# A fused attention and mixture-of-experts kernel: four chunks of pairs in place of five, and two expert blocks a slot behind the attention

## The chip, the cores and the metric

The kernel runs on one core of one Trainium2 chip. The metric is the device time of one execution in microseconds (us); lower is better. All data is float32. Each product is taken as three matmuls, of a high and a low part of either operand ("hi" and "lo"), so that every operand of TensorE is split first: ScalarE copies the hi part out of PSUM, VectorE subtracts it for the lo part.

## The reference, cut to what matters

Cross-attention over 64 sequences of 128 tokens and then a mixture of experts (two of eight for each token), both with a residual. Cut to the arithmetic:

```python
# attention: 64 sequences, 128 tokens, C = 256, 16 heads of 64
q = layernorm(x) @ Wq;  k, v = split(y @ Wkv)
x = x + softmax(q k^T * 64 ** -0.5) v @ Wproj + bproj
# experts: t = layernorm(x)
probs = softmax(t @ gate_w.T);  top2_w, top2_idx = top_k(probs, 2)
mixed = sum over the two chosen e of top2_w * silu(t @ expert_w[e].T + expert_b[e])
x = x + mixed @ combine_w.T
```

## The kernel before, in words

**Pairs and slots.** The 64 sequences are worked in 32 pairs (256 tokens each). The attention of a pair takes 8 slots, one for each pair of heads; slot s belongs to pair s // 8 and has u = s % 8. All engines walk the same list of slots in program order, each issuing its own part, and meet at semaphores. The attention fills slots 0 to 255; what comes from slot 256 on is called the tail here.

**Two ways through the experts.** The last four pairs (28 to 31) are "dense": all eight experts are computed for all their tokens, in 32 dense jobs (`plan.dense`, 8 a pair, up to 3 a slot, from slot 256 on). A dense job is 6 matmuls of 512 columns into one of four banks (`dense_ps`); ScalarE takes tanh and scales, VectorE multiplies (`dense_out`) and adds (`dense_add`), GpSimd adds (`add_odd`).

The first 28 pairs (`SPARSE`) are "sparse", in chunks of `CHUNKS` = 8, 8, 6, 4, 2 pairs. After the last pair of a chunk its rows lie sorted by expert in `sorted_x` (scattered by GpSimd), and a chunk of n pairs is worked in 4n + 7 blocks of 128 rows (`Plan.blocks`), the 7 being room for the padding of eight experts: 39, 39, 31, 23 and 15, together 147. `Plan.turn` gives each block a slot, one block a slot.

**A block turned in slot s:** SyncE loads its rows in slot s-2 (`load_rows`, 128 KB) and its expert's weights in s-1 (`load_expert`, 512 KB); TensorE turns the rows in slot s (`turn_block`, L714, 2 matmuls, "early" in the slot), the two splits go to `xbT`; in s+1 TensorE does 6 matmuls (`expert`, "late"); in s+2 ScalarE does tanh and VectorE `expert_out` (L1089) into `y_block`; in s+3 SyncE stores the block to `sorted_y` (`store_block`, L503). The rings of `x_block`, `w_block` and `y_block` have three places (`RING`), `xbT` has two. The waits of the rings: `load_rows(n)` on `turn_block` n-3, `load_expert(n)` on `expert` n-3, `expert_out(n)` on the landed store of block n-3.

**Mixing a sparse pair m:** when all blocks of its chunk are stored, GpSimd gathers four times (`gather`, indirect DMAs; two buffers, so that the first gather of pair m waits for `turn_mixed` of pair m-2), ScalarE weighs (`weigh`, L938), TensorE sums and turns (`turn_mixed`, L681, 8 matmuls) and one slot later multiplies (`combine`, 12 matmuls), VectorE adds the residual (`combined`, L1095) that SyncE has loaded back (`x1_back`), SyncE stores. `Plan.mix` gives the slot: mixes at s, `turn_mixed` in s+1, `combine` in s+2, `combined` in s+3.

**Banks.** All jobs beside the attention's own (`value`, `turn_x`, `turn_x1`, `gate`, `rank`, `turn_block`, `expert`, `turn_mixed`, `combine`) take three PSUM banks `gen_ps` in turn, in the order of `Plan.order`: a job waits until the job three before it is drained (`before_in_bank`).

**Order inside a slot of the tail.** TensorE: `turn_block`, then `turn_x1`/`gate`/`turn_mixed` ("mid"), then `expert`, `combine` ("late"), then the dense jobs. VectorE: `expert_out`, `combined`, then `dense_out` and `dense_add` of the dense jobs of slot s-1, then the lo splits of `turn_block` and of `turn_mixed`. GpSimd: `add_odd` of slot s-1's dense jobs and the gathers, alternately. SyncE: `load_rows`, `load_expert`, `store_block`, (the expert table for the dense jobs, 4 x 512 KB each, in slots 253 and 256: `load_experts`), the store of the output, the load of `x1_back`.

**The plan before, by slots:** blocks turned in 78 to 116, 142 to 180, 190 to 220, 222 to 244 and 245 to 259 (143 of them below slot 256, 4 in the tail; the chunks end with pairs 8, 16, 22, 26, 28, and behind each end VectorE computes the block list in the pair after the next). `turn_mixed` of pairs 0 to 21 lies below slot 256, of 22 to 27 in the tail, the last two (26, 27) mixed at slots 266 and 268. The last dense job stands in slot 267.

## Time and profile before

| | |
|---|---|
| median of the runs | 1540.31 us (1539.81 to 1540.96, 3 runs) |
| the profiled execution | 1538.33 us |
| its span, first to last instruction | 1536.6 us |
| PE (TensorE) busy | 1489.9 us, 97% |
| DVE (VectorE) busy | 1291.6 us, 84% |
| ACT (ScalarE) busy | 1061.8 us, 69% |
| POOL (GpSimd) busy | 939.1 us, 61% |
| granted TensorE clock | 0.996 of full speed |

The profile names instructions by line of the kernel, engine, and the tiles written and read. SP is SyncE. The tail is read from the order of time of each engine; for the attention, stretches of one pair each are read, each cut at the first of the four transposes of the probabilities (L636) that open a slot on TensorE. The names in the trace are those of the memory: `xT` and `v_s` can be the turned rows of a dense pair, `wq_s`, `wkv_s` the dense expert weights, and `x_kept` the kept residual.

### The profile page before, as it was taken

To read this page: it belongs to the slowest core of one execution; us is meant where nothing else is said; L and a number is where in the kernel's file an instruction comes from. 1 tells how busy PE (TensorE), PEld (TensorE's weight loads), DVE (VectorE), ACT (ScalarE), POOL (GpSimd) and SP (SyncE) were. 2 spreads that over 40 slices of the span, in tenths; PEclk is the share of its full clock that TensorE was granted. 3 is DMA by queue.
4 is the path that set the end of the run, shared out by engine and by line. 5 is a ranking of instruction groups with operands and counts; after the bars stand their busy time and mean duration, and the time that the engine had idled before them with its cause. 6 is when DMAs were issued, how large, how long until landed. Compare 5 with 4: busy or idle time off the path is not lost.

```text
span 1536.6 us, 38493 instructions
## 1 busy us (share of the span) xinstructions
PE 1489.9 (97%) x11680; PEld 1433.8 (93%) x11680; DVE 1291.6 (84%) x3129; ACT 1061.8 (69%) x2929; POOL 939.1 (61%) x1237
## 2 busy tenths in 40 slices
PE   6989999999999999999999999999999999999898
PEld 6989999999899999999999999989999999999887
DVE  7888888888988888888988888888888888987677
ACT  5766776766677667676677667766767667677665
POOL 4666666666655555587766455657666656655644
PEclk8999999999999999999999999999999999999999
DMA  6643443333577777544578777647887778887853
GB/s 183 201 152 94 108 110 97 94 94 97 162 226 209 220 217 223 159 114 140 172 230 244 217 231 232 203 117 220 243 250 237 230 228 248 251 243 216 285 183 110
DMA packets 181596, 287.78 MB, mean 187 GB/s; under 512 B 23697, under 2 KB 116881, under 8 KB 181137
## 3 DMA queue, kind: packets, MB, share of 16 engines
q1 hardware_dynamic: 170640, 255.94, 57.0%
q0 software_dynamic: 10752, 29.37, 6.1%
q8 instruction: 97, 1.59, 0.5%
q14 instruction: 107, 0.87, 0.2%
HBM read 156.51 MB, written 61.60 MB: 142 GB/s over the span
## 4 chain that ended last, share of the span: by engine, by line
PE 77%; DVE 14%; issue 3%; ACT 2%; SPq 2%; DMA 1%; POOL 0%; DVEq 0%; ACTq 0%; POOLq 0%
PE gen_ps L595 20%; PE qk_ps L595 17%; PE o_ps L595 10%; PE s_ps L595 10%; PE proj_ps L595 9%; PE pT_ps L636 6%; DVE sums L1073 2%; PE gen_ps L714 2%; PE gen_ps L681 2%; DVE neg_max L1066 2%; DVE pT_s_lo L1008 1%; DVE qk_s L1008 1%; PE gen_ps L689 1%; DMA k_s<-qk_s 1%; DVE xn L1053 1%
## 5 line engine op out<-in xcount | busy, mean ns | idle before, releaser
L851 ACT ACTIVATE stage<-s_ps,neg_max 128x128 f32<-128x128 f32 x1024 | 293.7, 376 | 32.1 <-DVE neg_max L1066 31.1
L1405 POOL CAST o_s_hi<-stage 128x256 fp32r<-128x256 f32 x256 | 102.5, 400 | 342.8 <-ACT stage L825 340.9
L1396 POOL TENSOR_TENSOR stage<-stage,inv_sums 128x512 f32<-128x512 f32 x256 | 266.1, 1039 | 36.8 <-DVE inv_sums L1075 36.4
L825 ACT CAST qk_s<-qk_ps 128x512 fp32r<-128x512 f32 x256 | 150.8, 589 | 134.3 <-PE qk_ps L595 132.7
L1066 DVE TENSOR_REDUCE neg_max<-s_ps 128x4 f32<-128x512 f32 x256 | 176.4, 689 | 66.6 <-PE s_ps L595 62.4
L595 PE MATMUL s_ps<-k_s,qk_s 128*128 128x256 f32 x1536 | 226.7, 284 | 2.8 <-DMA k_s<-qk_s 2.2
L1008 DVE TENSOR_TENSOR pT_s_lo<-pT_ps,pT_s_hi 128x512 fp32r<-128x512 f32 x256 | 173.7, 678 | 45.7 <-ACT pT_s_hi L825 41.4
L595 PEld LDWEIGHTS s_ps<-k_s,qk_s 128*128 128x128 f32 x1536 | 201.8, 189 | 3.5 <-DMA k_s<-qk_s 2.8
L1407 POOL TENSOR_TENSOR o_s_lo<-stage,o_s_hi 128x256 fp32r<-128x256 f32 x256 | 189.4, 740 | 20.8
L825 ACT CAST v_s_hi<-gen_ps 128x512 fp32r<-128x512 f32 x129 | 75.8, 588 | 179.4 <-PE gen_ps L595 179.4
L825 ACT CAST pT_s_hi<-pT_ps 128x512 fp32r<-128x512 f32 x256 | 150.4, 588 | 64.4 <-PE pT_ps L636 60.3
L1073 DVE TENSOR_REDUCE sums<-stage 128x4 f32<-128x512 f32 x256 | 172.6, 674 | 24.6 <-ACT stage L851 23.6
L825 ACT COPY stage<-o_ps 64x256 f32<-64x256 f32 x512 | 187.9, 367 | 3.1
L1008 DVE TENSOR_TENSOR qk_s<-qk_ps,qk_s 128x512 fp32r<-128x512 f32 x256 | 174.5, 681 | 0.5 <-ACT qk_s L825 0.4
L595 PE MATMUL o_ps<-pT_s_hi,v_s_hi 128*128 128x256 f32 x512 | 155.9, 304 | 18.7 <-DVE pT_s_lo L1008 18.4
L595 PE MATMUL qk_ps<-xT_hi,wq_s_hi 128*128 128x256 f32 x512 | 165.2, 323 | 7.9 <-DVE cT_hi L1060 4.0
L636 PE MATMUL pT_ps<-ident,stage 128*128 128x128 f32 x1024 | 154.5, 273 | 1.2 <-POOL stage L1396 1.1
L595 PE MATMUL proj_ps<-wproj_s_hi,o_s_hi 128*128 128x256 f32 x512 | 144.9, 283 | 2.0 <-POOL o_s_lo L1407 2.0
L595 PE MATMUL o_ps<-pT_s_hi,v_s_lo 128*128 128x256 f32 x512 | 145.2, 284 | 0.0
L595 PE MATMUL o_ps<-pT_s_lo,v_s_hi 128*128 128x256 f32 x512 | 144.7, 283 | 0.0
L595 PE MATMUL qk_ps<-xT_hi,wq_s_lo 128*128 128x256 f32 x512 | 144.7, 283 | 0.0
L595 PE MATMUL proj_ps<-wproj_s_hi,o_s_lo 128*128 128x256 f32 x512 | 144.3, 282 | 0.0
(385 smaller groups left out, 4695.2 us busy)
## 6 DMA issues: line engine op xcount, KB each, us to landing
w_block<-expert_table SPq DMA_DIRECT2D x147, 512.0 KB
k_s<-qk_s SPq DMA_DIRECT2D x512, 128.0 KB
stage<-sorted_x SPq DMA_DIRECT2D x147, 128.0 KB
sorted_y<-stage SPq DMA_DIRECT2D x147, 128.0 KB, 4.0
x_raw<-in_x SPq DMA_DIRECT2D x32, 256.0 KB
c_raw<-in_ctxT SPq DMA_DIRECT2D x32, 256.0 KB, 3.9
stage<-in_x SPq DMA_DIRECT2D x32, 256.0 KB, 3.7
x_kept<-x SPq DMA_DIRECT2D x32, 256.0 KB
```

The source lines that it names most:

```text
L595: mm = pe.matmul(out_ap, l, r, start=start and n == 0, stop=stop and n == len(terms) - 1, skip_group_check=skip)
L636: mm = pe.transpose(pT_ps[:, k * P:(k + 1) * P], probs[p % 2][:, k, :], ident[:, :])
L681: mm = pe.matmul(bank[:, a * N2 + t * P:a * N2 + (t + 1) * P], rows(t, k)[:, a * P:(a + 1) * P], ident[:, :], is_transpose=True, start=k = ...
L714: mm = pe.transpose(bank[:, a * P:(a + 1) * P], x_block[n % RING][:, a * P:(a + 1) * P], ident[:, :])
L825: last = act.copy(to, of)
L851: last = act.activation(probs[p % 2][:, k, :], s_ps[:, k * P:(k + 1) * P], ACT.Exp, bias=neg_max[p % 2][:, k:k + 1])
L1008: last = dve.tensor_tensor(lo, of, hi.bitcast(F32), ALU.subtract)
L1066: dve.tensor_reduce(neg_max[p % 2][:, :], s_ps[:, :].rearrange("p (k n) -> p k n", k=4), AX_X, ALU.max, negate=True).then_inc(max_done, 1)
L1073: dve.tensor_reduce(sums[p % 2][:, :], probs[p % 2][:, :, :], AX_X, ALU.add).then_inc(sums_done, 1)
L1396: pool.tensor_tensor(probs[b][:, :, :], probs[b][:, :, :], inv_sums[b][:, :].unsqueeze(2).broadcast_to([P, 4, P]), ALU.mult).then_inc(prob ...
L1405: pool.tensor_copy(hi[:, :, :], o_full).then_inc(o_hi, 1)
L1407: pool.tensor_tensor(lo[:, :, :], o_full, hi[:, :, :].bitcast(F32), ALU.subtract).then_inc(o_lo, 1)
```

## The change

The chunks are 9, 9, 7 and 3 pairs, so the blocks are 43, 43, 35 and 19, together 140. From slot 256 on the plan takes two blocks a slot. Blocks turned in slot 256 or later ("late") put their hi and lo parts in four places in `qk_s`, which the attention no longer uses, and not in the two of `xbT`. SyncE loads rows of late blocks one slot ahead and their weights in their own slot (before: two slots and one slot ahead), and in the tail stores the blocks of slot s-3 ahead of the loads rather than behind them. Everything else follows from `Plan`.

The new plan by slots: blocks turned in 86 to 128, 158 to 200, 214 to 248 and 249 to 261 (128 below slot 256; 12 in slots 256 to 261, two a slot). `turn_mixed` of pairs 0 to 17 below slot 256; pairs 18 to 27 in the tail, with mixes of 24, 31, 25, 26, 27 at slots 267, 268, 269, 271, 273. The last dense job stays in slot 267. The gathers of pairs 25, 26 and 27 stand in slots 266, 268 and 270.

The jobs on the three banks in the first slots of the tail, in order (before: `turn_block`, `turn_mixed` and `expert` of one block each in slot 256, for example):

```
256: turn_block 128, turn_block 129, turn_mixed, expert 127
257: turn_block 130, turn_block 131, expert 128, expert 129, combine
258: turn_block 132, turn_block 133, turn_mixed, expert 130, expert 131
259: turn_block 134, turn_block 135, expert 132, expert 133, combine
260: turn_block 136, turn_block 137, turn_x1, turn_mixed, expert 134, expert 135
261: turn_block 138, turn_block 139, gate, turn_mixed, expert 136, expert 137, combine
262: turn_mixed, expert 138, expert 139, combine
```

```diff
-CHUNKS = (8, 8, 6, 4, 2)
+CHUNKS = (9, 9, 7, 3)
...
             for b in range(self.blocks[c]):
-                self.turn[at] = (c, b, self.first[c] + b)
-                at += 1
+                while len(self.turn.get(at, [])) >= (1 if at < SLOTS * pairs else 2):
+                    at += 1
+                self.turn.setdefault(at, []).append((c, b, self.first[c] + b))
...
+        self.late_blocks = [n for at, jobs in self.turn.items() if at >= SLOTS * pairs for _, _, n in jobs]
...
+        late_xbT = [[qk_s[b // 2][:, b % 2, part, :].rearrange("p (a n) -> p a n", a=2) for part in range(2)] for b in range(4)]
+        turned = lambda n: late_xbT[n % 4] if n in plan.late_blocks else whole(xbT[n % 2])
...
-                if s + 2 in plan.turn:
-                    load_rows(*plan.turn[s + 2])
-                if s + 1 in plan.turn:
-                    load_expert(*plan.turn[s + 1])
-                if s - 3 in plan.turn:
-                    store_block(*plan.turn[s - 3])
+                if s - 3 >= SLOTS * pairs:
+                    for job in plan.turn.get(s - 3, []):
+                        store_block(*job)
+                for at, load, late in ((s + 2, load_rows, False), (s + 1, load_rows, True),
+                                       (s + 1, load_expert, False), (s, load_expert, True)):
+                    if (at >= SLOTS * pairs) == late:
+                        for job in plan.turn.get(at, []):
+                            load(*job)
+                if s - 3 < SLOTS * pairs:
+                    for job in plan.turn.get(s - 3, []):
+                        store_block(*job)
...
                     elif kind == "turn_block":
-                        wait(act, made["expert"], n - 1)
...
+                        if n not in plan.late_blocks:
+                            wait(act, made["expert"], n - 1)
+                        elif n - 4 in plan.late_blocks:
+                            act.wait_ge(made["expert"], n - 3)
+                        else:
+                            act.wait_ge(s_made, pairs * HEAD_PAIRS)
```

## Rows read from the trace of the kernel before

**Rows 1.** The page: span, and busy time of the engines.

```profile
span 1536.6 us, 38493 instructions
PE 1489.9 (97%) x11680; PEld 1433.8 (93%) x11680; DVE 1291.6 (84%) x3129; ACT 1061.8 (69%) x2929; POOL 939.1 (61%) x1237
```

**Rows 2.** Stretches, one pair each: length, PE, PEld, DVE, ACT, POOL busy, clock, DMA share, GB/s.

```profile
344.92:383.92 39.00, 38.22 (x305) 36.96 (x304) 33.84 (x80) 27.38 (x76) 24.98 (x34) 1.00 0.37 96
383.92:426.53 42.61, 40.21 (x314) 37.99 (x313) 38.81 (x104) 28.89 (x80) 25.23 (x34) 1.00 0.56 162
471.75:516.96 45.21, 45.21 (x368) 44.30 (x367) 38.72 (x97) 31.68 (x92) 25.16 (x34) 1.00 0.75 222
690.35:733.84 43.49, 42.70 (x345) 41.47 (x344) 35.82 (x85) 31.43 (x87) 32.99 (x43) 1.00 0.48 134
830.53:880.73 50.20, 50.05 (x408) 48.88 (x407) 41.64 (x101) 35.75 (x104) 25.45 (x35) 1.00 0.76 226
1304.65:1356.06 51.41, 50.25 (x406) 48.65 (x405) 44.96 (x114) 35.56 (x102) 33.24 (x43) 1.00 0.83 255
1406.23:1451.03 44.80, 42.87 (x354) 41.73 (x352) 33.00 (x81) 32.95 (x98) 26.32 (x35) 1.00 0.81 248
```

**Rows 3.** PE in order of time, tail: start, length, instruction, idle before it and releaser.

```profile
1453.57 0.41 PE L714 MATMUL gen_ps<-ident,stage 128*128 128x128 f32 x2 [1.94 <-DMA stage<-sorted_x]
...
1462.22 0.40 PE L595 MATMUL gen_ps<-w_block,xbT_hi 128*128 128x256 f32 x2
...
1462.94 0.28 PE L595 MATMUL gen_ps<-wcomb_s_hi,mT_s_hi 128*128 128x256 f32 x1
...
1464.36 0.39 PE L595 MATMUL pT_ps<-wq_s_hi,x1T_hi 128*128 128x512 f32 x1
...
1467.15 0.38 PE L714 MATMUL gen_ps<-ident,stage 128*128 128x128 f32 x2
...
1473.44 0.38 PE L714 MATMUL gen_ps<-ident,stage 128*128 128x128 f32 x2
1473.58 0.48 PE L595 MATMUL gen_ps<-w_block,xbT_hi 128*128 128x256 f32 x2
```

**Rows 4.** Page, costliest groups: a 128x512 copy out of PSUM on ScalarE (mean ns of one).

```profile
L825 ACT CAST pT_s_hi<-pT_ps 128x512 fp32r<-128x512 f32 x256 | 150.4, 588 | 64.4 <-PE pT_ps L636 60.3
```

**Rows 5.** VectorE in order of time, tail (columns as in Rows 3).

```profile
1455.15 0.42 DVE L1089 SCALAR_TENSOR_TENSOR stage<-stage,gen_ps 128x256 f32<-128x256 f32 x1 [2.12 <-DMA sorted_y<-stage]
...
1467.68 0.69 DVE L1095 TENSOR_TENSOR stage<-gen_ps,stage 128x512 f32<-128x512 f32 x1 [3.70 <-DMA stage<-x_kept]
...
1470.27 0.42 DVE L1008 TENSOR_TENSOR xbT_lo<-gen_ps,xbT_hi 128x256 fp32r<-128x256 f32 x1
```

**Rows 6.** SyncE in order of time, tail: loads of weights, of rows, stores.

```profile
1450.12 0.34 SPq L498 DMA_DIRECT2D w_block<-expert_table  x1
1450.50 0.46 SPq L503 DMA_DIRECT2D sorted_y<-stage  x1
1451.95 0.34 SPq L486 DMA_DIRECT2D stage<-sorted_x  x1
```

**Rows 7.** The stores of blocks (L503) from 1440 us on: issue to landing.

```profile
DMA to landing us min/median/max: 3.2/4.6/6.3
```

**Rows 8.** Stretches of one slot of the tail, columns as in Rows 2.

```profile
1451.03:1459.64 8.61, 6.67 (x47) 5.86 (x46) 3.64 (x10) 3.87 (x9) 4.81 (x7) 1.00 1.06 389
1473.44:1479.98 6.54, 6.54 (x40) 5.66 (x39) 4.80 (x10) 4.93 (x12) 5.55 (x7) 1.00 0.26 81
```

**Rows 9.** The end, by engine in order of time: last dense matmul, gathers, weighing, last addition.

```profile
1524.83 0.40 PE L595 MATMUL o_ps<-wkv_s_hi,v_s_lo 128*128 128x512 f32 x1
...
1518.80 0.95 POOL L1441 DMA_INDIRECT stage<-sorted_y,y_row_of  x1 [0.30 <-issue]
...
1525.76 1.69 ACT L938 ACTIVATE stage<-stage,top_w 128x256 f32<-128x256 f32 x4
...
1533.28 0.69 DVE L1095 TENSOR_TENSOR stage<-gen_ps,stage 128x512 f32<-128x512 f32 x1 [0.70 <-PE gen_ps L595]
```

More of the change, by code:

```diff
@@ L115, in __init__ @@
                     mid.append((kind, (i + off) * per(kind) + k))
-            if s in self.turn:
-                early.append(("turn_block", self.turn[s][2]))
+            for _, _, n in self.turn.get(s, []):
+                early.append(("turn_block", n))
             if s - 1 in self.mix:
                 mid.append(("turn_mixed", self.mix[s - 1]))
-            if s - 1 in self.turn:
-                late.append(("expert", self.turn[s - 1][2]))
+            for _, _, n in self.turn.get(s - 1, []):
+                late.append(("expert", n))
             if s - 2 in self.mix:
@@ L719, in expert @@
                 pe.wait_ge(w_block_in[n % RING], 16 * (n // RING + 1))
-                xs, w = xbT[n % 2], w_block[n % RING]
+                xs, w = turned(n), w_block[n % RING]
                 terms = []
@@ L901, in general @@
                     elif kind == "turn_block":
-                        wait(act, made["expert"], n - 1)
-                        to = xbT[n % 2][0][:, :, :].rearrange("p a n -> p (a n)")
-                        split_hi(made[kind], n + 1, [(to, bank[:, 0:N2])], hi_of[kind])
+                        if n not in plan.late_blocks:
[4 more added lines that the diff above has]
+                            act.wait_ge(s_made, pairs * HEAD_PAIRS)
+                        split_hi(made[kind], n + 1, [(turned(n)[0], bank[:, 0:N2].rearrange("p (a n) -> p a n", a=2))],
+                                 hi_of[kind])
                     elif kind == "turn_mixed":
@@ L963, in _ @@
                     pT(i, u - 1)
-                if s - 2 in plan.turn:
-                    tanh(plan.turn[s - 2][2])
+                for _, _, n in plan.turn.get(s - 2, []):
+                    tanh(n)
                 todo = plan.dense.get(s - 1, [])
@@ L1263, in general @@
                     elif kind == "turn_block":
-                        hi, lo = (y[:, :, :].rearrange("p a n -> p (a n)") for y in xbT[n % 2])
-                        split_lo(hi_of[kind], n + 1, [(lo, bank[:, 0:N2], hi)], drained[kind])
+                        hi, lo = turned(n)
+                        split_lo(hi_of[kind], n + 1, [(lo, bank[:, 0:N2].rearrange("p (a n) -> p a n", a=2), hi)], drained[kind])
                     elif kind == "gate":
@@ L1294, in _ @@
                     add_residual(i - 1)
-                if s - 2 in plan.turn:
-                    expert_out(plan.turn[s - 2][2])
+                for _, _, n in plan.turn.get(s - 2, []):
+                    expert_out(n)
                 if s - 3 in plan.mix:
```

## The prediction

> **What bounds the kernel now.** I read the page first, then stretches of one pair each, then each engine in order of time in the tail, and last the end.
>
> TensorE is busy 1489.9 of 1536.6 us [rows 1]. In the attention the stretches show it directly. A pair without blocks takes 39.00 us, one with 8 blocks 45.21 with PE busy for all of it, one with 2 mixes and no block 43.49, one with both 50.20 [rows 2]. So work taken from TensorE there shortens the kernel at its full price. The exceptions are the pairs in which VectorE computes a block list: 42.61 with two blocks, where 39.00 plus two blocks would be 40.6 [rows 2]; about 2 us are lost at each chunk end.
>
> The tail runs from 1451.03, the start of slot 256 [rows 8], to 1536.6, so 85.6 us. Its beginning is disturbed by DMA: share 1.06 and PE busy 6.67 of 8.61 us in slot 256, with a wait of 1.94 us for a block's rows; by slot 259 the share is 0.26 and PE is busy throughout [rows 3, 8]. The last dense matmul ends at 1524.83 + 0.40 = 1525.2 and 11.4 us of mixes, addition and output follow [rows 9].
>
> **Term 1, the attention.** The plan's counts with the stretches [rows 2] as prices. One block costs (45.21 - 39.00) / 8 = 0.78 us, two mixes 4.5 to 5.0. Pairs 8 to 31 last 1451.03 - 344.92 = 1106.1 us before. After, they are: two without anything (78.0), a chunk end with 2 blocks (42.6), five with 8 blocks (226.1), one with a single block (39.8), two with mixes only (87.0), a chunk end with 2 blocks and 2 mixes (42.6 + 4.5 = 47.1), one full (50.2), one with 8 blocks and a mix (47.7), three with 8 blocks (135.6), one with a block (39.8), a chunk end as above (47.1), two full (100.4), a chunk end with 8 blocks and 2 mixes (51.4), one with 8 blocks and a mix (47.7), and the last pair, which is 44.80 before and loses both mixes (39.8). Sum 1080.2, so -26. By parts: 15 blocks fewer are -11.6, four mixes -9 to -10, one chunk end -2, which is -23; the rest is from fewer slots in which blocks and mixes meet. I take -26, with -23 and -28 as bounds.
>
> **Term 2, work moved into the tail.** Eight blocks and four mixes more than before (12 blocks turned and 13 `expert` against 4 and 5; 10 sparse mixes against 6). A turn is 0.14 us (1473.44 to 1473.58), an `expert` 0.72 (1462.22 to 1462.94), a `combine` 1.42 (1462.94 to 1464.36), a mix as a whole 2.25 to 2.5 (half of the 4.5 to 5.0 above), which leaves some 0.87 for its `turn_mixed` [rows 2, 3]. Eight blocks are 6.9 us. Ahead of the end of the last dense job only one of the four mixes lies (0.87 + 1.42 = 2.3), the others fall behind it. So +9.2 up to there.
>
> **Term 3, the end.** Before, three `turn_mixed`/`combine` are still open behind the last dense job, and the last gather was issued at 1518.80, long before. After, pairs 24, 31, 25, 26 and 27 are open, and the gather of 26 waits for `turn_mixed` of 24, that of 27 for `turn_mixed` of 25, both behind the last dense job. Counted from its end: the last dense job's tanh (0.6, as the copy of the same shape [rows 4]), `dense_out` (0.7), scaling and `add_odd` stand ahead of the gather on GpSimd, 2.9 with a split between them; four gathers of 0.95 + 0.30 [rows 9] are 5.0, twice, so the last begins at 12; landing 3.5 (estimate from the stores' 3.2 to 4.6 [rows 7]); weighing 1.7; `turn_mixed` 1.1, the two splits 1.3 (0.59 and 0.69 [rows 4, 9]), `combine` 1.6; addition and output from 1533.28 to 1536.6, 3.3 [rows 9]. That is 24.7 against 11.4: +13.3. If the gathers were hidden only PE's work would count: 5 x 0.87 + 6 x 1.42 + 3.3 = 16.2, so +4.8. I take +13.3, because the waits are in the code and nothing is left that could cover them.
>
> Without new stalls the sum is -26 + 9.2 + 13.3 = -3.5.
>
> **Term 4, new waits of two blocks a slot.** Three banks and a job that waits for the third before it: with one block a slot `expert` waits for jobs of the slot before. With two, in slot 259, `expert` 133 waits until `turn_block` 134 of its own slot is drained; `turn_mixed` waits in the same way in 260 and 261, `combine` for `turn_mixed` in 262. The lo split that drains it stands on VectorE behind the dense jobs of the slot before. Rows: in slot 258, start 1467.15, it begins at 1470.27, 3.1 us in [rows 3, 5]; PE would need the bank after 1.0 us (two turns and one `expert`). Queued behind the waiting matmul are the dense jobs, so the stall is not hidden.
>
> How late is it? From `combined` at 1467.68 to that split are 2.6 us with two dense jobs, so 1.0 us a dense job [rows 5]. Lower bound: VectorE keeps up and only the last dense job is left at the slot's start (tanh 0.6, then 1.0, the addition of the job before it 0.4, the split 0.42): drained at 2.4, a stall of 1.4, four times, 5.5 us. Upper bound: VectorE is held by the ring of `y_block`. `expert_out` of a slot's second block needs the store that SyncE issues at the head of the same slot, and SyncE gets there only after the weights' load that waits for the first `expert` of the slot before. That load, a store and its next issues take 0.4 to 1.45 us each [rows 6], together about 2.5, and the store lands in 4.6 [rows 7]: 7.1 after that `expert`, where TensorE needs 0.7 + 4.2 (+1.4) = 4.9 to 6.3 to the next slot (the 4.2 are three dense jobs, two of them lasting from 1464.36 to 1467.15 [rows 3]). So `expert_out` is held 0.8 to 2.2 us into the slot and three dense jobs (3.0), the addition and the split follow: drained at 4.5 to 6, stalls of about 3.5, four times 14 us. The same kind of wait exists in slot 256 before, 2.12 us for `sorted_y` [rows 5].
>
> The first slots add to it. In 256 `turn_mixed` now waits for the bank that this `expert_out` (1455.15) drains, and the rows of the second block are asked for only one slot ahead in a full DMA: +2.5. In 258 `turn_mixed` waits for `combined`, which waited for `x_kept` until 1467.68 [rows 5]: +2.5. The four places for turned rows remove a wait that costs nothing here. Term 4 is then 10 to 19 us; I take 14.
>
> **A rule weighed.** The rows show stores landing in 3.2 to 6.3 us, median 4.6 [rows 7]. The Trainium skill (DMA: Bandwidth & Descriptors, Anatomy of one DMA) puts the fixed cost of a DMA at some 2 us, most of it the write's receipt. By that rule the store would land before it is missed and term 4 would be its lower bound, 10, so 1547; the rows were taken with the DMA engines full, as they will be here, so I go by the rows.
>
> **The sum.** -26 + 9.2 + 13.3 + 14 = +10.5 on the profiled execution's 1538.3 gives 1548.8. The median of the runs lies 2.0 above the profiled one: 1550.8, so 1551.
>
> **Rivals.**
> (B) The banks and the ring are hidden: VectorE and SyncE keep ahead and term 4 is 0 to 3. For it: VectorE has idle time in slot 258 (3.70) [rows 5] and is 84% busy in all [rows 1]. Against it: the order in which the lo split comes last. Time: 1540.3 - 3.5 + 1 = 1538; with term 1 at -28, 1536. This is the side "not slower".
> (C) The end isn't bound by gathers: term 3 is +4.8. Time with term 4: 1542; with a small term 4, 1530. For it: GpSimd is 61% busy [rows 1]. Against: the two waits named.
> (D) DMA binds. Eight blocks more are 8 x 768 KB = 6.3 MB. At slot 256's 389 GB/s with share 1.06 [rows 8] that is 16 us of full engines, against 8 us more of PE work. It decides if the loads of slots 256 to 259 (with the 2 MB of the expert table) aren't through by slot 260; weights then land late, and term 4 grows to about 24: 1561.
> That the change doesn't do what it says isn't a case for itself: the block count falls from 147 to 140 by the plan. If moved work were free in the tail, term 1 alone would stand, 1514; TensorE's full slots there [rows 8] exclude it.
>
> **Chances.** Forecast 0.52, B 0.20, C 0.13, D 0.15. About 0.2% (3.1 us) is what a measurement of this kernel can tell from no change. The forecast is slower but for 0.04; B is faster 0.08, same 0.11, slower 0.01; C 0.04, 0.04, 0.05; D slower. Together faster 0.12, same 0.19, slower 0.69. The range, 1537 to 1562, leaves out the low ends of B and C and the worst of D.
>
> **What would show it.** Term 1: slot 256 starts near 1425. Term 2: five slots from 256 with two `turn_block` each. Term 3: from the last dense matmul to the end some 25 us, with eight gathers in it one after the other. Term 4: in slots 259 to 262 idle time ahead of `gen_ps` matmuls, released by VectorE's `xbT` lo or by `expert_out`, and VectorE waiting for `sorted_y`. I am wrong if PE is as busy there as in slot 259 before, or if the end is as short as 16 us.

## The result, and the profile after

The changed kernel takes 1578.45 us (median of 4 runs, 1573.81 to 1582.06) against 1540.63 for the kernel before in the same session, a ratio of 1.0244 [1.0222, 1.0266]. So it is slower, as forecast, but by 38 us where 10.5 were forecast, and outside the range. The profiled execution took 1577.42 us, its span 1575.7. The rows of its page that answer to [rows 1]:

```profile
span 1575.7 us, 38156 instructions
PE 1500.7 (95%) x11624; PEld 1441.6 (91%) x11624; DVE 1282.6 (81%) x3096; ACT 1057.4 (67%) x2915; POOL 938.2 (60%) x1237
```

PE has 56 matmuls fewer and is busy 10.8 us longer. Something makes matmuls longer, which no step of the prediction provided for.

The span is cut here at three points: the first transposes of the probabilities in slot 24 (the start-up is over by then), those of slot 256, and the end of the last dense matmul. All values are us from the profiled executions. "Last gather" is the start of the last indirect DMA against the last dense matmul.

| kernel | slot 24 at | 24 to 256 | 256 to last dense | from there to the end | last gather | median | ratio to before |
|---|---|---|---|---|---|---|---|
| before | 149.9 | 1301.2 | 74.2 | 11.4 | -6.4 | 1540.6 | 1 |
| after | 156.0 | 1280.8 | 111.5 | 27.5 | +12.4 | 1578.45 | 1.0244 |
| forecast | as before | 1275 | 97.4 | 24.7 | +12 | 1551 | |
| e1 chunks only | 148.9 | 1279.9 | 92.8 | 36.1 | +23.5 | 1559.4 | 1.0129 |
| e5 two a slot only | 148.5 | 1304.8 | 85.3 | 11.7 | -27.1 | 1552.4 | 1.0080 |
| e2 output places | 155.4 | 1283.6 | 96.8 | 29.0 | +12.4 | 1558.4 | 1.0131 |
| e4 own banks | 149.2 | 1280.5 | 104.6 | 29.6 | +12.4 | 1565.6 | 1.0169 |
| e6 both | 152.1 | 1281.3 | 94.0 | 27.9 | +12.4 | 1549.9 | 1.0050 |
| e3 weights a slot later | 148.5 | 1281.7 | 117.6 | 27.2 | +12.4 | 1577.4 | 1.0249 |
| e7 e6, weight places | 149.7 | 1280.0 | 92.8 | 27.6 | +12.4 | 1551.4 | 1.0070 |
| e8 e7, gathers free | 155.4 | 1279.7 | 91.6 | 26.8 | +10.5 | 1555.7 | 1.0114 |
| e9 waits filled | 154.0 | 1280.8 | 117.5 | 27.9 | +12.4 | 1578.2 | 1.0247 |
| e10 9, 9, 6, 4 | 149.8 | 1289.9 | 87.2 | 16.9 | +3.0 | 1544.9 | 1.0023 |
| e11 the same, code before | 151.4 | 1290.5 | 78.3 | 29.9 | +13.5 | 1549.5 | 1.0050 |
| e12 e10, output places | 148.6 | 1288.2 | 85.9 | 16.9 | +3.0 | 1541.3 | 1.0001 |
| e13 e12, rows early, a stall | 150.9 | 1290.6 | 85.2 | 18.1 | +3.0 | 1545.8 | 1.0028 |
| e14 rows early, no stall | 150.1 | 1288.0 | 80.4 | 16.8 | +3.0 | 1539.1 | 0.9992 |

The attention gained 20.4 of the 26 us forecast. The stretch to the last dense matmul lost 37.3 (forecast 23.2), the end 16.1 (forecast 13.3). The start-up took 6.1 us more; that isn't the change (see the last section).

The stretch to the last dense matmul as one line, of before and then of after (length, PE, PEld, DVE, ACT, POOL busy, granted clock, DMA share, GB/s):

```profile
1451.03:1525.22 74.19, 70.83 (x414) 60.58 (x412) 55.83 (x115) 46.94 (x105) 38.54 (x48) 1.00 0.53 176
1436.75:1548.22 111.47, 91.51 (x500) 78.60 (x499) 61.83 (x133) 55.77 (x130) 44.76 (x54) 0.88 0.57 181
```

TensorE is idle there for 20.0 us in place of 3.4, and busy for 20.7 us more. So the 37.3 us are 16.6 of waiting and 20.7 of busy time; the second part is moved work and matmuls at a lower granted clock (below).

**The waits.** VectorE in order of time in the tail of after (start, length, instruction, idle before it and releaser), the lines that answer to the first of [rows 5]:

```profile
1459.38 0.42 DVE L1105 SCALAR_TENSOR_TENSOR stage<-stage,gen_ps 128x256 f32<-128x256 f32 x1 [9.65 <-DMA sorted_y<-stage]
1469.88 0.42 DVE L1105 SCALAR_TENSOR_TENSOR stage<-stage,gen_ps 128x256 f32<-128x256 f32 x1 [5.12 <-DMA sorted_y<-stage]
1480.82 0.42 DVE L1105 SCALAR_TENSOR_TENSOR stage<-stage,gen_ps 128x256 f32<-128x256 f32 x1 [2.53 <-DMA sorted_y<-stage]
1496.81 0.42 DVE L1105 SCALAR_TENSOR_TENSOR stage<-stage,gen_ps 128x256 f32<-128x256 f32 x1 [6.76 <-DMA sorted_y<-stage]
1510.21 0.42 DVE L1105 SCALAR_TENSOR_TENSOR stage<-stage,gen_ps 128x256 f32<-128x256 f32 x1 [3.69 <-DMA sorted_y<-stage]
```

`expert_out` stands and waits for the landed store of the block three before it: 27.8 us in five waits, where before had 2.8 in two. SyncE in order of time shows why the stores are late (answering to [rows 6]):

```profile
1452.59 0.34 SPq L504 DMA_DIRECT2D w_block<-expert_table  x1
1452.97 0.43 SPq L509 DMA_DIRECT2D sorted_y<-stage  x1
1454.17 3.76 SPq L492 DMA_DIRECT2D stage<-sorted_x  x2
1458.72 6.80 SPq L504 DMA_DIRECT2D w_block<-expert_table  x2
1465.56 0.43 SPq L509 DMA_DIRECT2D sorted_y<-stage  x1
```

The two weight loads take from 1458.72 to 1465.52, since the second waits for TensorE's `expert` three blocks back; the store stands behind it in the same queue. The first and longest of the five waits, 9.65 us, isn't of this kind: its store, issued at 1452.97, stood behind loads that waited for no `expert`, and took 6.31 us to land. The `expert` that holds the second weight load is in PE's list (columns as above):

```profile
1456.18 0.66 PE L725 MATMUL gen_ps<-ident,stage 128*128 128x128 f32 x2 [3.10 <-DMA stage<-sorted_x]
1459.85 0.69 PE L725 MATMUL gen_ps<-ident,stage 128*128 128x128 f32 x2 [3.01 <-DVE stage L1105]
...
1462.77 2.93 PE L606 MATMUL gen_ps<-w_block,qk_s 128*128 128x256 f32 x12 [0.35 <-DVE qk_s L1024]
...
1473.07 1.64 PE L606 MATMUL gen_ps<-w_block,qk_s 128*128 128x256 f32 x6 [2.27 <-DVE stage L1105]
1476.95 1.65 PE L606 MATMUL gen_ps<-w_block,qk_s 128*128 128x256 f32 x6 [2.23 <-DVE qk_s L1024]
```

TensorE waits for L1105, which is `expert_out` again. That closes a circle: `expert` frees the weights' place, SyncE issues the load and only then the store, the store lands, `expert_out` runs and drains the bank, the next `turn_block` and `expert` run. The first `expert` of a slot starts at 1462.77, 1473.07, 1487.99, 1502.78 and 1512.68. The four periods between (columns as in the fence of the whole stretch):

```profile
1462.77:1473.07 10.30, 8.03 (x34) 6.69 (x34) 2.77 (x9) 2.70 (x6) 6.26 (x8) 0.83 0.66 215
1473.07:1487.99 14.92, 11.29 (x59) 9.89 (x59) 10.71 (x22) 8.18 (x20) 3.18 (x4) 0.77 0.45 127
1487.99:1502.78 14.79, 9.81 (x54) 8.61 (x52) 5.85 (x14) 4.78 (x11) 5.44 (x6) 0.80 0.60 195
1502.78:1512.68 9.90, 9.90 (x53) 9.04 (x51) 3.58 (x7) 5.13 (x12) 0.96 (x2) 0.77 0.38 124
```

TensorE is idle for 2.3, 3.6, 5.0 and 0.0 us of them, and in each about 2 us of its busy time are there because the clock is low (busy time times what is missing of the clock, an estimate). The remaining 6 to 9 us are work. Only the first and the third period go over the weights and a store. In the second the chain that ended last runs over VectorE instead: the multiplications and additions of the dense jobs stand ahead of the lo split of the turned rows (`qk_s`, L1024) that TensorE waits for, 2.23 and 1.40 us. That is the wait that term 4 described.

**The clock.** Stretches of 10 us of after (length, PE, PEld, DVE, ACT, POOL busy, granted clock, DMA share, GB/s):

```profile
1446.70:1456.70 10.00, 6.70 (x41) 5.41 (x39) 2.45 (x7) 4.04 (x11) 1.36 (x2) 0.97 1.08 362
1456.70:1466.70 10.00, 6.64 (x27) 5.57 (x27) 5.27 (x13) 2.80 (x7) 1.62 (x3) 0.52 0.43 141
1466.70:1476.70 10.00, 5.74 (x26) 4.32 (x24) 4.46 (x9) 4.25 (x11) 6.27 (x7) 0.82 0.96 303
1496.70:1506.70 10.00, 7.42 (x34) 7.33 (x35) 5.84 (x13) 5.04 (x13) 2.37 (x3) 0.52 0.16 54
```

Behind the stretches in which TensorE idles, the granted clock falls to 0.52, close to the lower of the two levels (1.2 of 2.4 GHz), and 27 matmuls keep PE busy for 6.64 us where 41 took 6.70 in the stretch ahead. The twelve matmuls of two `expert` at 1462.77 took 2.93 us; at the full clock two take 0.87 and 0.95. This is the likely source of the 10.8 us more of PE busy time: busy time times what is missing of the clock comes to some 9.6 us up to the last dense matmul and 2.5 behind it, where before has nothing (an estimate). Whether that busy time is also lost time is what e9 asks.

### The profile page after: what moved, and what is told of

The parts are those of the page before. It is cut to its first block, busy times and chain, and to the rows that moved or that the text cites. A ratio compares the mean times of both kernels' runs of the same rounds, so it can differ in the third digit from the quotient of the medians.

```text
span 1575.7 us, 38156 instructions
## 1 busy us (share of the span) xinstructions
PE 1500.7 (95%) x11624; PEld 1441.6 (91%) x11624; DVE 1282.6 (81%) x3096; ACT 1057.4 (67%) x2915; POOL 938.2 (60%) x1237
## 4 chain that ended last, share of the span: by engine, by line
PE 75%; DVE 13%; issue 4%; DMA 3%; ACT 2%; SPq 2%; POOL 1%; DVEq 0%; ACTq 0%; POOLq 0%
PE gen_ps L606 19%; PE qk_ps L606 17%; PE o_ps L606 10%; PE s_ps L606 10%; PE proj_ps L606 9%; PE pT_ps L647 6%; PE gen_ps L725 2%; PE gen_ps L692 2%; DVE sums L1089 2%; DVE neg_max L1082 1%; DVE pT_s_lo L1024 1%; DVE qk_s L1024 1%; DMA k_s<-qk_s 1%; PE gen_ps L700 1%; DVE xn L1069 1%
## 5 line engine op out<-in xcount | busy, mean ns | idle before, releaser
L862 ACT ACTIVATE stage<-s_ps,neg_max 128x128 f32<-128x128 f32 x1024 | 292.9, 375 | 29.6 <-DVE neg_max L1082 28.5
L1024 DVE TENSOR_TENSOR pT_s_lo<-pT_ps,pT_s_hi 128x512 fp32r<-128x512 f32 x256 | 173.5, 678 | 44.0 <-ACT pT_s_hi L836 39.3
L1024 DVE TENSOR_TENSOR qk_s<-qk_ps,qk_s 128x512 fp32r<-128x512 f32 x256 | 174.3, 681 | 0.4 <-ACT qk_s L836 0.4
L606 PE MATMUL qk_ps<-xT_lo,wq_s_hi 128*128 128x256 f32 x512 | 144.4, 282 | 0.0
```

Source lines behind the costliest of these rows:

```text
L606: mm = pe.matmul(out_ap, l, r, start=start and n == 0, stop=stop and n == len(terms) - 1, skip_group_check=skip)
L862: last = act.activation(probs[p % 2][:, k, :], s_ps[:, k * P:(k + 1) * P], ACT.Exp, bias=neg_max[p % 2][:, k:k + 1])
L1024: last = dve.tensor_tensor(lo, of, hi.bitcast(F32), ALU.subtract)
```

## The experiments

**e1 and e5: each half of the change alone.** e1 is the code before with the new chunks, e5 the changed code with the old chunks.

```diff
-CHUNKS = (8, 8, 6, 4, 2)
+CHUNKS = (9, 9, 7, 3)
```

> The kernel before with the chunks 9, 9, 7, 3 and nothing else: one block a slot in the tail too. Theory R (the ring of y_block with two blocks a slot makes the tail slow): VectorE no longer waits for sorted_y by more than some 3 us in all, the tail up to the last dense job is 74 + 9 = 83 us in place of 111.5, the end is longer (the last block is stored in slot 270, then three pairs are gathered): some 30 us. Attention as in the changed kernel. Total 1545 to 1552. Theory P (the chunk plan itself, more mixes and gathers in the tail, makes it slow): 1565 or more.

> The changed kernel with the old chunks 8, 8, 6, 4, 2: two blocks a slot only for the four blocks of slots 256 and 257. Theory R (ring of y_block) and B (banks) both: few slots have two blocks, so 2 to 8 us of new waits; the attention as before (T, the start of slot 256, at 1451 in a run with the short start), the end not longer than 11.4 us because pairs 26 and 27 are mixed earlier. Total 1541 to 1548. If two blocks a slot cost nothing by themselves: 1540 or less.

The chunks alone bring the whole gain in the attention (1279.9) and lose it in the tail: 92.8 and 36.1, since one block a slot ends in slot 267 and the last gather comes 23.5 us behind the last dense matmul. The median, 1559.4, lies between the two theories (1552 at most, 1565 at least): VectorE waits for stores 0.6 us only, as theory R has it, but TensorE waits seven times, 6.8 us in all, for the lo split of the turned rows (`xbT_lo`), which neither theory had. Two blocks a slot alone cost 11.1 us up to the last dense matmul (2 to 8 were expected) though only four blocks are late. VectorE's waits for stores there, in e5:

```profile
DVE stage L1105 <- DMA sorted_y<-stage: 10.8, 3, 9.0
```

(us in total, times, longest). TensorE itself waits twice there, 5.3 us for this `expert_out` and 3.4 for rows. So the ring is the larger part of the price of two a slot, and not all of it; and both halves are slower than before. What the second half buys is the end: 27.5 in place of 36.1.

**e2, e4, e6: the ring and the banks.** e2 gives the outputs of the 12 late blocks places of their own in `k_s`, so that `expert_out` waits for no store. e4 takes the late `turn_block` from slot 258 on out of the three banks, into halves of `proj_ps`. e6 is both.

```diff
+        y_late = [k_s[b][:, h, part, :] for b in range(AHEAD) for h in range(2) for part in range(2)]
...
-                wait(dve, y_stored[n % RING], 16 * (n // RING))
+                if n in plan.late_blocks:
+                    dve.wait_ge(s_made, pairs * HEAD_PAIRS)
+                else:
+                    wait(dve, y_stored[n % RING], 16 * (n // RING))
```
```diff
+            if plan.own_bank((kind, n)):
+                return proj_ps[:, (n % 2) * N2:(n % 2 + 1) * N2]
```

> The changed kernel, but the outputs of the 12 late blocks have a place each in the keys' buffers, so that expert_out waits for no store (these outputs are rounded to the matmul's input format, which changes no work). Theory R: the 28 us that VectorE waits for sorted_y vanish; the tail falls from 139 to 110 to 115 us, total 1550 to 1555. Theory B (the bank coupling of turn_block and expert inside a slot is the cause): 5 us at most are gained, total 1572 or more, with the idle time of TensorE now all released by the lo split.

> The changed kernel, but the turned rows of late blocks from slot 258 on use the two halves of the projection's bank, which is free by then, so that no expert or turn_mixed waits for a turn_block of its own slot. Theory B: 15 us or more gained, total 1563 or less. Theory R: 2 to 6 us gained, total 1572 to 1576, and VectorE's waits for sorted_y stay near 28 us.

> The changed kernel with both of the edits tried one at a time: own places for the outputs of late blocks, and the projection's bank for their turned rows from slot 258 on. If ring and banks are two separate delays: T to the last dense matmul falls from 111.5 to 88 to 92 us (the work alone needs 83), total 1548 to 1552. If one is only behind the other in the same chain: no better than the places alone, 96.8 us and 1556 or more.

Up to the last dense matmul: 111.5, with places 96.8, with banks 104.6, with both 94.0. So the ring is worth 14.7 alone and 10.6 on top of the banks, the banks 6.9 alone and 2.8 on top of the places. Together 17.5 us of the 37.3. With the waits goes the low clock: in e6 TensorE is idle for 10.1 us and busy for 83.9, at a granted clock of 0.98, so that 7.6 of the 17.5 us are busy time. e2 and e6 fell short of what was expected of them (a median of 1558.4 against 1550 to 1555, and 94.0 us against 88 to 92). Each is a link of the circle; taking out either shortens it, the ring much more.

**e3: the order on SyncE.** The second block's weights are loaded a slot later, behind the stores and the rows.

```diff
+                if s - 1 >= SLOTS * pairs:
+                    for job in plan.turn.get(s - 1, [])[1:]:
+                        load_expert(*job)
```

> The changed kernel, but SyncE issues the weights of a slot's second late block one slot later, behind the stores and the loads of rows, so that a store no longer stands behind a load that waits for TensorE's expert. The ring of y_block keeps three places. Theory R in its narrower form (the store waits in SyncE's queue): 12 to 20 us gained, total 1558 to 1566. If the landing of the stores is what counts: under 5 us gained. Theory B: nothing.

TensorE's waits in its tail:

```profile
PE gen_ps L612 <- DMA w_block<-expert_table: 15.9, 4, 7.3
```

The store no longer stands behind the weights, but now the weights come late: 117.6, and none of the 12 to 20 us expected is gained. The order alone moves the wait and doesn't take it away. I put that down to the rings, with three places where two blocks a slot want more under way; no run shows it by itself.

**e7 and e8: the weights' ring and the gathers.** e7 adds eight places for late weights to e6. e8 adds to that a place of its own for pair 26's gathered rows, so that the gathers of 26 wait for no `turn_mixed`, and issues those of 26 one slot and of 27 two slots earlier.

```diff
-                    if m >= 2:
-                        pool.wait_ge(made["turn_mixed"], plan.turn_of[m - 2] + 1)
+                    if m >= 2 and m != SPARSE - 2:
+                        pool.wait_ge(made["turn_mixed"], plan.turn_of[m - (3 if m == SPARSE - 1 else 2)] + 1)
```

> As e6, and the weights of the late blocks in eight places (three of w_block, the third part of qk_s, four in the projection's weights) in place of three, so that SyncE's loads wait for no expert of the slot before. If the order of SyncE still holds the tail: 3 to 6 us less than e6, T to the last dense matmul at 84 to 86. If DMA bandwidth holds the first slots: no change against e6.

> As e7, and pair 26 is gathered into the place of x_block (free by then) one slot earlier, pair 27 two slots earlier into pair 26's place, so that neither waits for a turn_mixed behind the last dense job. If the end is bound by gathers one after the other: from the last dense matmul to the end 29 falls to 20 to 23 us, total 6 to 8 us below e7. If TensorE or the splits bind the end: 2 us or less.

e7 moves the stretch by 1.2 us (3 to 6 were expected) and the median not at all: with the outputs free, the weights were hardly late. e8, expected at 20 to 23 us for the end and measured at 26.8, is the miss that tells most about it. Its last dense matmul ends at 1526.70, and GpSimd in order of time is

```profile
1519.60 0.97 POOL L1509 DMA_INDIRECT stage<-sorted_y,y_row_of  x1 [4.37 <-PE gen_ps L732]
1520.59 0.75 POOL L1519 TENSOR_TENSOR last_row<-last_row,stage 128x256 f32<-128x256 f32 x1
...
1532.58 0.73 POOL L1519 TENSOR_TENSOR zero_rows<-zero_rows,c_raw 128x256 f32<-128x256 f32 x1
...
1537.25 0.94 POOL L1509 DMA_INDIRECT stage<-sorted_y,y_row_of  x1 [0.30 <-issue]
```

From 1519.60 on GpSimd has no pause: 12 gathers and six additions stand in one line, and the last gather still starts 10.5 us behind the last dense matmul. The earlier gathers now stand ahead of the additions that the last dense pair needs, and PE waits for the one at 1532.58. So at the end it is GpSimd's queue that binds, not the wait that was removed.

**e9: is the low clock a cause?** 90 matmuls whose results nobody reads are put into TensorE's waits of the tail.

```diff
+                for _ in range(count):
+                    pe.matmul(to[:, 0:2 * C], wcomb_s[0][:, 0, 0:P],
+                              wcomb_s[0][:, :, :].rearrange("p a n -> p (a n)"), start=True, stop=True)
```

> The changed kernel with matmuls that compute nothing used put into TensorE's waits of the tail: 11 ahead of turn_block 132 and of turn_block 133 (slot 258), 8 ahead of expert 132 and of expert 133 (slot 259), 5 ahead of turn_mixed in slot 260, 11 ahead of the gate and 7 ahead of turn_mixed in slot 261, and behind the dense jobs 3, 10 and 10 ahead of the last three turn_mixed and 6 and 6 ahead of the last two combines; 90 matmuls of 512 columns, some 0.235 us each at the full clock (dense jobs of the trace: six from 1546.65 to 1548.06), 21 us in all, each lot a little shorter than the wait in which it lies. Theory 'the low clock is part of the circle': in the changed kernel TensorE's granted clock falls to 0.52 in 1456.7 to 1466.7 and in 1496.7 to 1506.7, 0.82 and 0.84 between; its busy time times what is missing from 1 gives 3.2 + 1.0 + 1.4 + 3.6 = 9 us of real work lengthened. With the waits filled the clock stays near 1 and slot 256 to the last dense matmul goes from 111.5 to about 102, and the end (clock 0.76 and 0.84) from 27.5 to about 25.5: median 1567. Rival 'the clock is only a trace of the waits': the work in the clock's low stretches is hidden behind the waits for stores and banks, and the fillers at best cost nothing: 111 to 116 us and 27 to 29, median 1578 to 1584.

Stretches of e9, the first two for those of after at 0.52 and 0.82:

```profile
1454.80:1464.80 10.00, 7.77 (x38) 5.63 (x36) 3.19 (x7) 2.20 (x7) 0.00 (x0) 1.00 0.83 290
1464.80:1474.80 10.00, 8.12 (x42) 6.60 (x42) 2.62 (x9) 2.36 (x5) 6.25 (x8) 1.00 0.68 223
1494.80:1504.80 10.00, 7.62 (x37) 5.88 (x36) 4.74 (x11) 1.93 (x5) 1.66 (x2) 0.83 0.42 154
```

The clock stays at the full level in the first two periods and falls again later (0.90 and 0.81 in the third and fourth). In sum nothing is gained: 117.5 us, of which 3.2 are a longer wait for rows in slot 256, where nothing was filled (4.78 against 1.59). The four periods are 10.1, 13.6, 15.9 and 9.5 us against 10.3, 14.9, 14.8 and 9.9 in after.

- The first shows that the low clock isn't what made it long: at the full clock it is as long as before, since VectorE waits for a store until 1474.59, and the `expert` that needs the bank starts at 1475.07.
- The second is 1.3 us shorter, the third 1.1 longer; there VectorE waited 7.91 us for a store, where it waited 6.76 in after.
- In the fourth TensorE waits for nothing in either run, and the clock is low in both (0.81 and 0.77). What a full clock would give there, e9 doesn't show.
- Behind the last dense matmul e9 is no test. Ten fillers stand ahead of the last `turn_mixed`, where after has no wait, and two lots of fillers, 2.28 and 2.31 us, lie on the chain that ended last. That the end is as long as in after (27.9 against 27.5) can be a shorter end with fillers in it.

So the low clock isn't the main cause of the waits. What it costs by itself stays open: it isn't shown to be free.

**e10, e11, e12: the third chunk one pair shorter.** Chunks of 9, 9, 6 and 4 have the same 140 blocks, but the third chunk's 31 blocks start in slot 206, not 35 in slot 214, so only 5 blocks are late and not 12. e10 is the changed code, e11 the code before, e12 is e10 with the output places of e2.

```diff
-CHUNKS = (9, 9, 7, 3)
+CHUNKS = (9, 9, 6, 4)
```

> The changed code with chunks of 9, 9, 6 and 4 pairs in place of 9, 9, 7 and 3. The same 140 blocks, but the third chunk ends a pair earlier, so only 5 blocks are left for the tail (slots 256 to 258, of which 256 and 257 take two) instead of 12, and 20 pairs are mixed below slot 256 instead of 18; the gathers of pair 27 stand in slot 267, its mix in 270 (before: 268). Theory 'what costs is how much is late and how late': attention -13 by the prices of the stretches (8 blocks fewer 6.2, two mixes 4.7, a chunk end 2), of which experience with 9, 9, 7, 3 leaves about -10; to the last dense matmul +3 of work (one block 0.9, about one mix 2.3) and +4 of waits in the two double slots; the end +3 to +6 for mixes that stand two slots later. Sum 0 to +3: 1540 to 1543. Rival 'the fourth chunk and the code behind it cost by themselves' (two blocks a slot at the full price of the run with two a slot alone, +12 to the last dense matmul, and an end of 25 us or more): 1555 or more.

> The code before (one block a slot) with chunks of 9, 9, 6 and 4: 140 blocks, 5 in the tail, one a slot in 256 to 260. The mix of pair 27 stands in slot 273, five slots later than before, and the gathers of 25, 26 and 27 in 266, 268 and 270. Attention -10 as in the run above. To the last dense matmul +3 of work and no ring or bank waits. Theory 'the end is bound by when the last gathers come': last gather about 12 us behind the last dense matmul and an end near 27 as in the changed kernel, +16; sum +9: 1549. Rival 'the end only follows from its work' (two mixes more behind the dense jobs, some 5 us): 1539.

> As the changed code with chunks 9, 9, 6, 4, and with places of their own for the outputs of the five late blocks (rounded to the type of those places), so that VectorE's expert_out waits for no store in the tail. With 9, 9, 7, 3 these places were worth 14.7 us to the last dense matmul, for 12 late blocks and five waits. Here only the waits at the first double slots are left to remove: the theory of the ring gives -2 to -5 against the run without them. If the ring matters only where doubles follow each other for six slots: no difference, within 1 us.

e10 came near what the first theory said (1540 to 1543): 1544.9, within 5 us of the kernel before and 34 us below the changed kernel. e11 shows what two blocks a slot are good for: it wins 8.9 us up to the last dense matmul against e10 and loses 13 at the end, with the last gather at +13.5 in place of +3.0. e12 takes 1.3 us off that stretch and 3.6 off the median; the first is less than I expected (2 to 5), since TensorE's waits for rows grew from 4.6 us in e10 to 8.0 as those for `expert_out` went.

**e13 and e14: what the rows wait for.** In e12 TensorE (first fence) waits twice for rows, and SyncE (second fence) had issued the rows of the first wait behind the table of the dense experts:

```profile
1442.09 1.09 PE L728 MATMUL gen_ps<-ident,stage 128*128 128x128 f32 x4 [4.72 <-DMA stage<-sorted_x]
...
1460.84 0.41 PE L728 MATMUL gen_ps<-ident,stage 128*128 128x128 f32 x2 [3.30 <-DMA stage<-sorted_x]
```
```profile
1426.34 0.39 SPq L524 DMA_DIRECT2D wq_s_hi<-expert_table  x1
...
1434.25 1.47 SPq L494 DMA_DIRECT2D stage<-sorted_x  x2
```

Both runs load the late rows earlier, in free places. The lines are those of e14; e13 asked for four of the rows in slot 253 and for the fifth in slot 254.

```diff
+                if s == SLOTS * pairs - 3:
+                    for job in plan.turn[SLOTS * pairs]:
+                        load_rows(*job)
+                if s == SLOTS * pairs - 1:
+                    for job in plan.turn[SLOTS * pairs + 1] + plan.turn[SLOTS * pairs + 2]:
+                        load_rows(*job)
```

> As the run with chunks 9, 9, 6, 4 and places for the outputs, and with the rows of the late blocks loaded before the 2 MB of the dense experts' table and not behind it: blocks 135 to 138 in slot 253, 139 in slot 254, in places of x_block whose blocks are turned by then and in the place of the chosen experts' masks, which is free after the last block list. Theory 'the rows queue behind the table': in the run without it the rows of 135 and 136 were issued at 1434.25, behind the four loads of the table from 1426.34 on, and TensorE waited 4.72 us for them at 1442.09; those of 139 were issued behind the second half of the table and TensorE waited 3.30 us at 1460.84. Both waits go; the weights that follow in the same full queues may give 1 to 3 of the 8 us back. Slot 256 to the last dense matmul from 85.9 to 79 to 81 us; median 1534.5 to 1537, which is faster than the kernel before. Rival 'the engines of DMA are the bound in slots 253 to 258, whatever the order': the weights come as much later as the rows come earlier, 84 to 87 us and 1540 to 1542.

> The run with the rows early again, without the wait that spoilt it. There SyncE asked in slot 253 for a place of x_block whose block is only turned in slot 254; it stood in the rows' load from 1426.85 to 1435.63 and issued the table at 1437.33 instead of 1426.34, and TensorE then waited 8.20 us for the first late block's weights' work. Now the rows of 135 and 136 go in slot 253, ahead of the table, to the place of the chosen experts' masks, with no wait, and those of 137, 138 and 139 in slot 255, where block 134 has been turned by the time SyncE comes there (1432.59 against 1434.25). Theory 'the rows queue behind the table': the waits of 4.72 and 3.30 us go, some 1 to 3 come back as waits for weights; slot 256 to the last dense matmul 79 to 82 us against 85.9, median 1535 to 1538, ratio about 0.997. Rival 'DMA is the bound in slots 253 to 258': 84 to 87 us, 1540 to 1542, ratio 1.000.

e13 fell into the trap that it was to study. SyncE of e13, then of e14:

```profile
1426.85 8.78 SPq L501 DMA_DIRECT2D stage<-sorted_x  x5
...
1437.33 0.39 SPq L532 DMA_DIRECT2D wq_s_hi<-expert_table  x1
```
```profile
1425.05 2.59 SPq L501 DMA_DIRECT2D stage<-sorted_x  x3
...
1429.35 0.39 SPq L532 DMA_DIRECT2D wq_s_hi<-expert_table  x1
```

One of the five loads of e13 asked for a place whose block was turned a slot later, and the table moved back by 11 us behind it. Without that stall, e14 goes from slot 256 to the last dense matmul in 80.4 us (expected 79 to 82; e12 85.9), and no wait of TensorE for rows is left there (one of 3.62 us for `expert_out` in slot 256 is). The bytes to be moved are the same in both runs, so what the rows of e12 waited for was their place in the order, not the bandwidth. The median, 1539.14, ratio 0.9992 [0.9977, 1.0006], is 1 us above what was expected and can't be told from the kernel before: long chunks can be had at no loss, but I found no version that is faster.

## Why the prediction was wrong, point by point

**Term 1, attention: right in kind, 5.6 us too high.** 20.4 of 26. Slot 256 came at 1436.7, or 1430.6 counted without the late start-up, against 1425 forecast. Two stretches of after for [rows 2], columns as there (the pair for which 45.21 was used, and one with everything):

```profile
1063.00:1108.16 45.16, 45.16 (x369) 44.26 (x367) 38.73 (x97) 31.65 (x92) 25.16 (x34) 1.00 0.77 221
1195.78:1246.01 50.23, 50.08 (x408) 48.86 (x407) 41.53 (x100) 35.19 (x100) 33.38 (x43) 1.00 0.79 239
```

The prices held. The excess lies in pairs to which I gave the price of an undisturbed one: 40.9, 40.7 and 40.9 where a single block was put at 39.8, and 48.4 and 52.0 at chunk ends put at 47.1 and 51.4; together 4.9.

**Term 2, moved work: some 2 us too low.** TensorE's busy time in the stretch, at the full clock, is 70.8 us before and about 82 after (91.5 less the 9.6 above; e7, with a clock of 0.98, is at 83.4). That is 11 us of work against 9.2, by an estimate.

**Term 4, the waits: this is the step that failed.** 37.3 - 9.2 leaves 28 where term 4 had 14. What the runs show in its place has two parts.

The idle time itself came near: 16.6 us more than before, against 14. It isn't spread as forecast. "Stalls of about 3.5, four times" are idle times of 2.3, 3.6, 5.0 and 0.0 us, and from slot 256 up to the first of them TensorE was idle for 8.4 us, where the 3.4 of before and the 5 forecast for the first slots make the same. The mechanism was named rightly: `expert_out` held by the landed store, which SyncE issues behind the load that waits for `expert`, and the lo split behind the dense jobs. That the sum nearly fits is in part luck: the fourth stall didn't come, the third was longer, and VectorE's longest wait, 9.65 us, was for a store that took 6.31 us to land and had no `expert` in its way. A part of the two in the middle isn't explained by a run: in both, a job of pair 31 (`turn_x1`, `gate`) and a `turn_mixed` stand in the order of the banks too.

The larger part of what is missing is a term that the prediction put at nothing: it priced the matmuls behind each wait as if TensorE kept its clock. They ran at a granted clock of 0.77 to 0.83 in the four periods, and came to some 9.6 us of busy time; with the 2 us of term 2 that makes the 28. e2 and e6 show that this goes when the waits go (busy 85.0 and 83.9 us in place of 91.5). How much of the 9.6 would have come back as waiting at a full clock is open (e9).

The rule weighed (the Trainium skill, DMA: Bandwidth & Descriptors, Anatomy of one DMA) would have taken the sum further off. Its fixed cost of some 2 us is fitted for DMAs issued by GpSimd, and these stores are issued by SyncE; the stores of the trace of before, at 3.2 to 6.3 us [rows 7], were the better guide.

The rows of the first late blocks were put at 2.5 us. They cost 3.10 + 1.59 in after and 8.0 in e12, and e14 shows the cause in e12, the table ahead of them in the queue. I had looked at rival D as bandwidth; for the rows it isn't that.

**Term 3, the end: right, 2.8 us short.** GpSimd and PE of after:

```profile
1551.15 0.97 POOL L1457 DMA_INDIRECT stage<-sorted_y,y_row_of  x1
1553.12 0.94 POOL L1457 DMA_INDIRECT stage<-sorted_y,y_row_of  x1 [1.01 <-issue]
...
1560.63 0.95 POOL L1457 DMA_INDIRECT stage<-sorted_y,y_row_of  x1 [0.30 <-issue]
```
```profile
1561.42 1.54 PE L692 MATMUL gen_ps<-ident,stage 128*128 128x128 f32 x8 [2.52 <-ACT stage L954]
...
1570.69 0.36 PE L606 MATMUL gen_ps<-wcomb_s_hi,pT_s_hi 128*128 128x256 f32 x1 [1.57 <-DVE pT_s_lo L1024]
```

The first gather starts 2.9 behind the last dense matmul (1548.22), as worked out, the last at 12.4 (12). The missing 2.8 lie behind it; `turn_mixed` takes 1.54 where 1.1 was taken, at a lower clock (0.87 over the whole end). The parts of the prediction's sum, as written, add to 24.5 and not 24.7. The reason given, the waits for `turn_mixed`, was only half of it: e8 removed them and GpSimd's own queue kept the last gather at 10.5.

**Rivals.** B fell: the banks and the ring were not hidden. C fell: the end follows the last gather (+3.0 and 16.9 us in e10 and e12, +13.5 and 29.9 in e11). D's 1561 was passed, too, but nothing shows DMA as the bound behind the first slots: the DMA share is 0.38 to 0.66 in the four periods.

## What to carry to other kernels

When a change adds a wait, follow it round before pricing it: the thing waited for can hang, over a queue worked in order, on the instruction that waits. And a wait has a price beside its idle time, if the matmuls behind it run at a lower granted clock; here that was 9.6 us of busy time beside 16.6 of idle time. Count the places of each ring against what the new schedule has under way at once: two blocks a slot with a store three slots later need more than the three places that one block a slot needed. And cut chunks by where the last one falls, not by how few blocks there are: one pair moved from the third chunk to the fourth was worth 34 us.

## What the runs showed of the hardware that was not expected

The granted clock fell to 0.52 behind stretches in which TensorE stood idle for 3 us at a time (3.10 and 3.01), and was 1.00 in the same part of e9, where matmuls of no use filled the waits. In the last of the four periods of after TensorE waited for nothing, and the clock was still 0.77.

The start-up, until slot 24, took from 148.5 to 156.0 us in the profiled executions, in kernels whose instructions there are the same. In after PE waited at 54.83 for 3.48 us on the keys' turn through DMA (`k_s<-qk_s`), where before waited 0.62 at 51.14, and its granted clock from 40 to 64 us was 0.86 where before had 1.00. Runs of the kernel before spread from 1537.3 to 1548.3 in one session. A difference of a few us between two single executions says nothing until the start-up is taken off.
